# A one-core transformer layer: another order of the work between attention and routing, and another split of the final combination

## The reference

```python
h = layernorm(x) * (1 + ca) + sa
x = x + ga * (softmax(rope(h @ Wq) @ rope(h @ Wk).T / 4) @ (h @ Wv)) @ Wo   # 16 heads, 4 of K and V
h = layernorm(x) * (1 + cb) + sb
shared = (silu(h @ Wg.T) * (h @ Wu.T)) @ Wd.T * sigmoid(h @ shared_gate.T)  # 704 wide
weights, sel = top_k(softmax(h @ gate.T), 4)                                # 60 experts
sparse = sum over the 4 choices of weight * ((silu(h @ A_e.T) * (h @ B_e.T)) @ C_e.T)   # 176 wide
out = x + gb * (shared + sparse)
```

## Time and profile before

| | us |
|---|---|
| median of 3 runs | 524.89 |
| lowest and highest | 522.38, 528.10 |
| the profiled execution's own time | 527.01 |
| its span, first to last instruction | 525.2 |
| TensorE busy | 467.3 (89%) |
| VectorE busy | 344.1 (66%) |
| ScalarE busy | 217.1 (41%) |
| Pool busy | 208.3 (40%) |

### The profile page before, as it was taken

The page is one execution under the profiler, slowest core; times in us unless marked ns, Lnnn a source line. Parts: engine busy times, 40 slices in busy tenths (PEclk is TensorE's granted clock), DMA queues, the critical chain, the costliest instruction groups (busy, mean ns, idle before and its releaser), DMA issues.

```text
span 525.2 us, 7847 instructions
## 1 busy us (share of the span) xinstructions
PE 467.3 (89%) x2748; PEld 250.5 (48%) x2748; DVE 344.1 (66%) x751; ACT 217.1 (41%) x317; POOL 208.3 (40%) x209
## 2 busy tenths in 40 slices
PE   3958889999999999997896999899999998999890
PEld 3635222333333333223664767566666666666560
DVE  5597959999999999902276973655545454455247
ACT  1547437878878788794213231111111111111140
POOL 3366000212032021200312244567777777776503
PEclk9987769999999999999597999999999999999996
DMA  8970000000000000000101001068888888884181
GB/s 282 337 216 0 1 0 2 1 1 1 1 2 1 1 2 2 0 1 1 40 0 41 1 1 29 13 198 256 271 258 252 244 265 244 278 262 146 38 338 61
DMA packets 33617, 53.68 MB, mean 102 GB/s; under 512 B 6870, under 2 KB 21918, under 8 KB 33584
## 3 DMA queue, kind: packets, MB, share of 16 engines
q1 hardware_dynamic: 27728, 44.82, 26.8%
q0 software_dynamic: 5856, 8.43, 5.6%
HBM read 50.71 MB, written 10.09 MB: 116 GB/s over the span
## 4 chain that ended last, share of the span: by engine, by line
PE 58%; DVE 18%; DMA 9%; issue 6%; POOL 5%; ACT 4%; SPq 0%; DVEq 0%; POOLq 0%; ACTq 0%
PE PV L1221 12%; DMA ychoice<-QS,tab 8%; PE M L1175 7%; PE EP L1403 7%; PE EP L1208 5%; PE EP L1211 5%; PE EP L1299 4%; DVE mx L788 2%; POOL QS L449 2%; PE PV L1420 2%; DVE x L1056 2%; POOL ychoice L454 2%; PE M L1420 1%; DMA x<-in_x 1%; DVE QS L1008 1%
## 5 line engine op out<-in xcount | busy, mean ns | idle before, releaser
L788 DVE TENSOR_REDUCE mx<-M 128x1 f32<-128x512 f32 x256 | 159.3, 683 | 18.0 <-PE M L1175 17.8
L607 ACT ACTIVATE QS<-EP 128x1024 f32<-128x1024 f32 x128 | 123.9, 1021 | 24.9 <-PE EP L1211 24.6
L1403 PE MATMUL EP<-w,QS 128*128 128x352 f32 x244 | 85.2, 472 | 1.3 <-DVE QS L997 1.3
L659 ACT ACTIVATE QS<-EP 128x176 f32<-128x176 f32 x61 | 19.3, 317 | 138.7 <-PE EP L1403 138.7
L449 POOL DMA_INDIRECT QS<-h2rows,tab x61 | 63.1, 1035 | 31.0 <-issue 13.2
L454 POOL DMA_INDIRECT ychoice<-QS,tab x61 | 61.8, 1013 | 21.9 <-issue 15.9
L1221 PE MATMUL PV<-QS,VA 128*32 128x512 f32 x512 | 69.7, 617 | 0.0
L997 DVE COPY QS<-EP 128x256 f32<-128x256 f32 x61 | 25.7, 422 | 63.7 <-PE EP L1397 63.7
L1175 PE MATMUL M<-KT,QT 64*128 64x512 bf16 x256 | 61.9, 403 | 3.5 <-DVE mx L788 2.6
L1403 PEld LDWEIGHTS EP<-w,QS 128*128 128x128 f32 x244 | 43.4, 189 | 26.5 <-issue 11.0
L1208 PE MATMUL EP<-QT,KT 64*128 64x512 bf16 x256 | 49.6, 380 | 1.6 <-ACT QTB L564 1.2
(11 more groups left out here) (240 smaller groups left out, 640.9 us busy)
## 6 DMA issues: line engine op xcount, KB each, us to landing
w<-in_w SPq DMA_DIRECT2D x30, 704.0 KB
w<-in_w SPq DMA_DIRECT2D x61, 112.0 KB
w<-ychoice SPq DMA_DIRECT2D x8, 512.0 KB, 8.3
w<-in_w SPq DMA_DIRECT2D x30, 128.0 KB
segu<-in_segu SPq DMA_DIRECT2D x1, 1408.0 KB, 10.7
x<-in_x SPq DMA_DIRECT2D x2, 512.0 KB, 5.1
wide<-in_wmod SPq DMA_DIRECT2D x1, 1024.0 KB, 8.3
h2rows<-xh SPq DMA_DIRECT2D x2, 512.0 KB, 2.9
```

Of the source, the lines that this page charges most:

```text
L607: nc.scalar.activation(PT[n % 3][:, 2 * p:2 * p + 2, :], EP[p][:, :, :], ACT.Exp, scale=HD ** -0.5).then_inc(e_done, 1)
L788: nc.vector.tensor_reduce(out=mx[:, u % 2, s // 2, j, s % 2:s % 2 + 1], in_=src, axis=AX.X, op=ALU.max).then_inc(m_free, 1)
L1403: ins = mm(BANK[b][:, 0:I13], XGT[b][:, c * P:(c + 1) * P], w13[:, r, c * I13:(c + 1) * I13], start=c == 0, stop=c == NC - 1)
```

## The change

On TensorE the last product with V and its transposes come right behind the attention, then the attention's transposes 2 and 3 (into banks 1 and 2), then the first half's rows, projections 2 and 3, the first logits and the shared expert's first half of tile 0; the second half's rows and logits follow. VectorE does `take_output` inside the first `second_norm`, both `second_norm`s one after the other, and then both routers. Pool does both powers before it scales the rows. At the end tile 3 goes from VectorE to ScalarE and Pool, and VectorE, ScalarE take the shared tiles and the combination in another order; the shared output of tile 7 is added last.

```diff
--- before.py
+++ after.py
@@ -68,10 +68,10 @@
         fills += half
     EARLY = NT - 2
 
-    AT_BANK, WO_BANK, H2_BANK = (4, 5, 5, 7), (7, 4, 4, 5), (5, 7, 7, 4)
+    AT_BANK, WO_BANK, H2_BANK = (4, 5, 1, 2), (7, 4, 4, 5), (5, 7, 7, 4)
 
     NB = NE + MAXOV
-    POOL_TILES = (2, 5)
+    POOL_TILES = (2, 3, 5)
 
     ctx = ExitStack()
     with ctx:
@@ -434,7 +434,8 @@
                 tt = slice(4 * h, 4 * h + 4)
                 pool.wait_ge(s_var2, h + 1)
                 pool.tensor_tensor(rstd[:, tt], veps[:, tt], mhalf[:, 0:4], ALU.pow).then_inc(s_rstd, 1)
-
+            for h in range(2):
+                tt = slice(4 * h, 4 * h + 4)
                 pool.wait_ge(s_tr2, 2 * h + 2)
                 pool.tensor_tensor(xh[:, tt, 0:D], xh[:, tt, 0:D], MOD[:, 4:5, :].to_broadcast([P, 4, D]), ALU.mult).then_inc(s_xm, 1)
                 pool.wait_ge(s_xm, 2 * h + 1)
@@ -610,14 +611,14 @@
                 if n in (STEPS - 4, STEPS - 3):
                     attention_T(n - STEPS + 4)
             take_sums(U - 1)
+            attention_T(2)
+            attention_T(3)
             act.wait_ge(s_mod1, 1)
             rows_T2(0)
             rows_T2(1)
-            router_exp(0)
-            attention_T(2)
-            attention_T(3)
             act.wait_ge(s_gate, 1)
             nc.scalar.activation(shg.rearrange("p (a n) -> p a n", a=2), EP[0][:, :, 0:SHH], ACT.Copy).then_inc(s_raw, 1)
+            router_exp(0)
             rows_T2(2)
             rows_T2(3)
             router_exp(1)
@@ -672,15 +673,18 @@
                     act.wait_ge(m_gu, i + (NE + 1))
                     act.wait_ge(m_h, i + NE)
                     nc.scalar.activation(SL[0], BANK[0][:, 0:I], ACT.Silu).then_inc(m_silu, 1)
-            for t in range(EARLY, NT):
-                shared_silu(t)
-                if t > EARLY:
-                    shared_evac(t - 1)
-            shared_evac(NT - 1)
-            for t in POOL_TILES:
+            def weighted(t):
                 act.wait_ge(s_yg[t], 16)
                 for k in range(TOPK):
                     nc.scalar.activation(YG[t][:, k, :], YG[t][:, k, :], ACT.Copy, scale=top[:, t, k:k + 1]).then_inc(s_weighted, 1)
+
+            shared_silu(NT - 2)
+            shared_silu(NT - 1)
+            shared_evac(NT - 2)
+            weighted(POOL_TILES[0])
+            weighted(POOL_TILES[1])
+            shared_evac(NT - 1)
+            weighted(POOL_TILES[2])
 
 
         @block.vector
@@ -799,7 +803,7 @@
             def take_output():
                 g, qh = q_unit(U - 1)
                 take()
-                o = BANK[4].rearrange("p (t j c) -> p t j c", t=4, j=4)
+                o = BANK[0].rearrange("p (t j c) -> p t j c", t=4, j=4)
                 then(nc.vector.reciprocal(rsum[:, 0], o[:, :, :, HD]))
                 nc.vector.tensor_tensor(AT[:, 4 * qh:4 * qh + 4, 4 * HD * g:4 * HD * (g + 1)].rearrange("p t (j d) -> p t j d", j=4),
                                         o[:, :, :, 0:HD], rsum[:, 0].unsqueeze(3).to_broadcast([P, 4, 4, HD]), ALU.mult).then_inc(m_free, 1)
@@ -844,6 +848,8 @@
                                             BANK[WO_BANK[tp]].rearrange("p (t n) -> p t n", t=2), ALU.add).then_inc(s_x1, 1)
                 dve.wait_ge(s_x1, 2 * h + 2)
                 statistics(h, s_var2)
+                if h == 0:
+                    take_output()
                 dve.wait_ge(s_rstd, h + 3)
                 normalise(h, s_h2)
 
@@ -895,9 +901,8 @@
 
             dve.wait_ge(s_iota, 6)
             second_norm(0)
-            take_output()
+            second_norm(1)
             router(0)
-            second_norm(1)
             router(1)
             then(nc.vector.tensor_scalar(sgate[:, 1, :], sgate[:, 0, :], 1.0, None, ALU.add))
             then(nc.vector.reciprocal(sgate[:, 0, :], sgate[:, 1, :]))
@@ -1048,29 +1053,30 @@
                     result(i + NE, 0, i * 16 + 16 * (NE // BUFS))
 
 
-            def combine(tiles):
+            def combine(tiles, ends=True):
                 for t in tiles:
                     dve.wait_ge(s_yg[t], 16)
                 for k in range(TOPK):
                     for t in tiles:
                         ins = nc.vector.scalar_tensor_tensor(out=x[:, t, :], in0=YG[t][:, k, :], scalar=top[:, t, k:k + 1],
                                                              in1=x[:, t, :], op0=ALU.mult, op1=ALU.add)
-                        if k == TOPK - 1:
+                        if k == TOPK - 1 and (ends or t < NT - 1):
                             ins.then_inc(s_fin, 1)
-                    if k < TOPK - 1:
+                    if k < TOPK - 1 or not ends:
                         then(ins)
 
-            for t in range(EARLY, NT):
-                shared_mul(t)
+            shared_mul(NT - 2)
             dve.wait_ge(s_base, 1)
             combine((0, 1))
-            for t in range(EARLY, NT):
-                shared_out(t)
-                dve.wait_ge(s_sh, t + 1)
-                then(nc.vector.tensor_tensor(x[:, t, :], x[:, t, :], SH[:, t, :], ALU.add))
-            combine((3, 4))
-            combine((6,))
-            combine((7,))
+            shared_mul(NT - 1)
+            shared_out(NT - 2)
+            dve.wait_ge(s_sh, NT - 1)
+            then(nc.vector.tensor_tensor(x[:, NT - 2, :], x[:, NT - 2, :], SH[:, NT - 2, :], ALU.add))
+            combine((4,))
+            combine((6, 7), ends=False)
+            shared_out(NT - 1)
+            dve.wait_ge(s_sh, NT)
+            nc.vector.tensor_tensor(x[:, NT - 1, :], x[:, NT - 1, :], SH[:, NT - 1, :], ALU.add).then_inc(s_fin, 1)
 
 
         @block.tensor
@@ -1191,7 +1197,7 @@
                 pe.wait_ge(s_atev, u + 1)
                 b = fill(a_free if u < U - 1 else m_free)
                 if u == U - 1:
-                    b = BANK[4]
+                    b = BANK[0]
                 for t in range(4):
                     ins = tr(b[:, t * P:(t + 1) * P], OT[:, t * P:(t + 1) * P], I_)
                 ins.then_inc(m_fill, 1)
@@ -1280,10 +1286,16 @@
                     attention_T(n - STEPS + 4)
                 if n in (STEPS - 2, STEPS - 1):
                     project(n - STEPS + 2)
+            output(STEPS - 1)
+            transpose_output(U - 1)
+            pe.wait_ge(m_free, took.count(m_free))
+            attention_T(2)
+            attention_T(3)
             rows_T2(0)
             rows_T2(1)
-            output(STEPS - 1)
-            transpose_output(U - 1)
+            project(2)
+            pe.wait_ge(s_tr2ev, 1)
+            project(3)
 
             def logits(tiles):
                 for t in tiles:
@@ -1307,21 +1319,16 @@
 
             pe.wait_ge(ld_wr, 16)
             logits(range(NT // 2)).then_inc(s_lg, 1)
-            pe.wait_ge(m_free, took.count(m_free))
-            attention_T(2)
-            attention_T(3)
             pe.wait_ge(ld_sh, 48)
             shared_half(0, 0, 0)
-            project(2)
-            project(3)
             shared_half(0, 0, 1).then_inc(s_gate, 1)
+            rows_T2(2)
+            rows_T2(3)
             shared_in(0, 1, s_up)
+            logits(range(NT // 2, NT)).then_inc(s_lg, 1)
             pe.wait_ge(s_raw, 1)
             shared_half(1, 0, 0)
-            rows_T2(2)
-            rows_T2(3)
             shared_half(1, 0, 1).then_inc(s_gate, 1)
-            logits(range(NT // 2, NT)).then_inc(s_lg, 1)
 
             def ranks():
```

## The result

The changed kernel took 519.67 us in the median of 13 runs (515.42 to 522.92) against 525.68 before (13 runs). The ratio is 0.9882 with a 95% interval of 0.9848 to 0.9916: faster by 1.2%, 6.0 us by the medians. The forecast was 518, in a range of 512.5 to 521.8. The profiled execution took 519.67 with a span of 517.9, 7.3 less than the span before.

What follows compares the result with a forecast made beforehand. Waits between TensorE and VectorE after the attention, Pool in the expert loop and VectorE's combination at the end were taken as bounds. Winning 3.3 and 3.5 us, 6.8 off the median 524.89, gave 518; range 512.5 to 521.8.

Steps and rivals of the forecast that it cites:

- The working's two halves, 3.3 and 3.5: Microseconds won by the new order after the attention (3.3) and by the new end (3.5).
- Projections: After the attention, projections 2 and 3 follow the first rows' transposes at once, ending at 256.2; one row began at 264.28 before.
- The term of 2.6 us: Cost taken off the front: TensorE's clock falls to 0.50, slowing the first rows' transposes and projections 2 and 3.
- the first rival: After the attention TensorE's clock holds, so 2.6 us fall away: 9.4 us won, 515.5; chance 0.22.
- 10.7 from 288.44: Time from routing 1's start (277.78) to the ranks (288.44), taken as unchanged in the new order.
- Pool beside VectorE: In routing 0, VectorE instructions with two SBUF inputs wait for Pool's long instructions, costing 3.0 us.
- my bound of 3.6: Upper bound, with 0 the lower, on what Pool's long instructions cost VectorE in routing 0.
- The end: Combination of tiles after the loop: 3.5 us won, with bounds of 2.4 and 5.9.
- The price of 0.85: At the end, one VectorE combining instruction takes 0.85 us while Pool combines too, 0.43 afterwards.
- The rival in which the end wins nothing: At the end a VectorE and Pool pair costs 1.28 us: 2.2 lost there, 523.8 in all; chance 0.15.
- The loop passed the gain on: The expert loop, paced by Pool, shifts as a whole, so the gain before the ranks passes undiminished.
- The slower rival: TensorE's low clock lasts past the ranks; with 12 us of such work 9.8 lost, 527.9; chance 0.04.

Runs made afterwards that it cites:

- experiment 4: The changed kernel's front with the end of the kernel before; ratio 0.9954 (0.9915 to 0.9992) to the kernel before.
- Experiment 9: The kernel of experiment 2 plus 18 unread products of 512 columns on TensorE behind the second half's shared products; ratio 0.9739 to the kernel before.
- experiment 1: The changed kernel with Pool's long instructions for the first half's rows again between the two powers; ratio 0.9841 to the kernel before.
- experiment 2: As experiment 1, with Pool's second-half long instructions also waiting for routing 0's mask; first chip ratio 0.9796, second chip 511.46 us, ratio 0.9743 to the kernel before.
- experiment 3: As experiment 2, but Pool's second-half long instructions wait for both routing masks; ratio 0.9837 to the kernel before.
- experiment 6: The changed kernel with tile 3 back on VectorE, so two Pool tiles in the new order; ratio 0.9893 to the kernel before.
- experiment 7: The changed kernel with three Pool tiles but the old order of the end on VectorE and ScalarE; ratio 0.995 to the kernel before.
- Experiment 8: The kernel of experiment 2 with no tile on Pool, VectorE combining all eight; 513.52 us, ratio 0.9805 to the kernel before.
- experiment 10: The changed kernel run again unaltered, on the chip of the later runs; ratio 0.989 (0.9851 to 0.9929) to the kernel before.

## Why the prediction held, and where its terms were wrong

*Time and sign.* Forecast 518, measured 519.67, and 6.8 us won by the working against 7.3 between the two spans and 6.0 between the medians. The working's two halves, 3.3 and 3.5, were measured as 3.76 and 3.68. But that the front's figure was right is luck: two terms were wrong in opposite senses, and the two executions lie at the favourable ends of the clock's scatter (some 2.6 us between the means of all, 2.5 in experiment 4).

*Projections.* As predicted, they follow the first rows' transposes, and VectorE's second add comes at 255.56. The last output on VectorE (0.25 and 0.42 us) was hidden under Pool's power.

*The clock.* The term of 2.6 us was 0 in this trace, where the clock held through both projections: the first rival. In five of eleven executions the clock fell, as the row at 56.06 had suggested, but it was back as the projections began and cost some 0.9 us (39.55 against 38.61) or 1.0 (32.87 against 31.84). So the fall is open from execution to execution, and the size was too large in both cases. What decides it no run here tells. The clock also came back earlier behind the second idle piece: eight shared products took 3.59 us where the row at 283.70 had 4.74, and the ranks stood 9.4 us behind routing 1's start in place of 10.5. (I had carried over 10.7 from 288.44, which is a later product of the ranks; the first is at 288.27.) Experiment 9 shows that below this nothing more is to be had, for the mask bounds it.

*Pool beside VectorE.* The mechanism was right and its extent wrong. The step that failed is "In routing 0 the instruction at the place of L880 and the four of L891 read two tensors from SBUF as that one does; the others read one, or PSUM": I let only those wait, and looked only at routing 0, though by my own times Pool's instructions began at 260.1 and the normalisation ended at 261.5. The normalisation, which has one tensor as its input and two columns as its scalars, waited for both of Pool's instructions, 4.1 us: its four instructions took 2.43, 2.50, 0.40 and 0.40, the first two ending 0.15 us behind one of Pool's each. The cast waited too. The product at L880's place did not (0.41), for Pool's other two instructions stood behind TensorE's transposes and came only at 267.03, which I had left out. With 2.6 us in routing 0 this is 6.7 where I took 3.0, outside my bound of 3.6. Experiments 1 to 3 show the cause by moving nothing but Pool's instructions: the waits follow them to whatever VectorE does beside them. The page "SBUF — State Buffer" of the Trainium skill, section "Who interferes with whom", names `copy`, `cast` and `tensor_scalar` among the VectorE instructions that can take the shared port. The traces agree: 5.49 for 1.38, 0.69 for 0.18 and 1.38 for 0.16. I had weighed only its sentence on two inputs.

*The end.* 3.5 predicted, 3.68 measured. The price of 0.85 for a VectorE instruction beside Pool's was right (0.86), and Pool ended at 513.57 with VectorE at 515.74, 2.2 us apart (1.9 predicted). But the working never asked what the order alone would do. Experiments 6 and 7 show that it is nearly the whole gain, and that the third Pool tile adds none in the new order: VectorE starts with tiles 0 and 1 2.1 us earlier, works while it used to wait 2.4 us for the last down product, and that product's result is added last. Experiment 8 shows why the tile adds none: at 0.86 us a pair Pool's help costs VectorE about what it spares it. I had the price and didn't draw this from it. The rival in which the end wins nothing is out: three tiles in the new order gave 26.8 to 27.2 us in seven executions and 28.2 in one, the old order 30.7 to 30.9 in three.

*Loop and late clock.* The loop passed the gain on (0.40 us longer here, 0.02 shorter in experiment 2 on the second chip). It scatters, though: 206.1 to 206.9 us in seven executions off the first chip, 208.45 in experiment 7 for no known reason, and 210.1 in experiment 3, where the slots' 3.0 us lie in it. The slower rival didn't happen: TensorE was back at full clock behind the ranks (eight shared products in 2.61 us).

## What to carry to other kernels

Before an instruction on Pool is moved, look at what VectorE does beside its new place, and let everything in SBUF count that a trace doesn't show free, a tensor_scalar or a cast with one input too; here moving four long Pool instructions to where VectorE waits or reads PSUM was worth 8.0 us between the medians of one chip (519.43 and 511.46, experiments 10 and 2; 6.8 us of the way to the ranks in two traces in which the clock held), more than the whole change (6.0). A split of work between VectorE and Pool should be tried without the split: 12 of 32 instructions taken off VectorE shortened the end by 1.0 us, and reordering them by 3.7. The two numbers to compare are the time of a pair, one instruction on each engine beside each other, and twice the time of one on VectorE alone: here 0.86 and 0.90. Two terms of opposite error can make a right sum, so each is worth its own look in the new trace; and a term that hangs on the clock is worth a second execution, for here the same kernel had it both ways.

## What the runs showed of the hardware that was not expected

- Four VectorE tensor_scalar instructions with one 128x256 tensor input each took 5.49 us beside two Pool tensor_tensor of 2.34 us, which themselves were not slowed; alone they take 1.38. It was 5.48 or 5.49 in all five executions with this placing. Where VectorE's instructions had started first, under routing 0, Pool's took 2.46 and 2.60 in place of 2.34.
- A VectorE scalar_tensor_tensor on 128x256 beside Pool's tensor_tensor on 128x256 came every 0.86 us, alone every 0.45; Pool's took 0.78 to 0.91 beside these and 0.72 while VectorE idled.
- A cast of 128x32 took 0.69 to 0.70 us beside Pool and 0.18 alone; a tensor_scalar of 128x7 took 1.38 and 0.16. Instructions that read PSUM (0.40), the reduction of 128x240 (0.40) and the search for the largest (0.59 for four) kept their times beside Pool.
- The granted clock stayed at 1.00 over 4.2 us in which TensorE was 1.77 us busy, with transposes, and in a repeat of the same kernel it was 0.50 for 3.4 us in the same place.
- One chip ran the kernel before 29.0 us slower than another (552.81 and 523.83) and the kernel of experiment 2 28.6 us slower (540.06 and 511.46); of the latter's traces, 26.4 us apart, 26.3 us lie between the ranks and the end of the expert loop.
